# Three late chunks, a shorter gathered part of layer 2, and its chunk transfers on ScalarE's queue

## Chip, cores and metric

The kernel runs on one core of a Trainium2 chip. The metric is the device time of one execution in microseconds (us). Before the change the median of three runs is 3162.39 us (3161.69 to 3169.01).

## What is computed

A graph of 6250 nodes with 206250 edges, sorted by destination, goes through two graph convolutions and a projection, and then each node goes through a mixture of eight experts, two for each node:

```python
deg_out = segment_sum(edge_weight, src); deg_in = segment_sum(edge_weight, dst)
norm = edge_weight * rsqrt(deg_out[src] * deg_in[dst] + EPS)
def gcn_layer(x, W, b):
    xt = x @ W                                        # 256 x 256
    agg = segment_sum(xt[src] * norm[:, None], dst)
    return relu(agg + b)
h6 = gcn_layer(layernorm(x), W6, b6)
h7 = gcn_layer(h6, W7, b7)
x = x + h7 @ Wp + bp
...
xn = layernorm(layernorm(x)) * gamma + beta           # then top 2 of 8 experts
y += (gelu(xn @ W1[e] + b1[e]) @ W2[e] + b2[e]) * weight_of_e
return x + y
```

All of it is float32.

## The kernel before

**Tiles, chunks and groups.** The sorted edges are cut into tiles of 128; eight tiles are a group, 202 groups in all. A layer's weighted sum over edges is made in two ways. The *gathered part*: for a group, GpSimd gathers the source rows of the table of the layer, one indirect DMA for each tile (L977, `gathers`), into a ring of four group buffers (`RING`). TensorE multiplies them with one-hot matrices from VectorE (`sums`, L2111) and, after each second group, adds up the rows of both in `combine` (L2124), for which it needs the copy of the sums by ScalarE (`copy_sums`, L1760) and one row that SyncE fetches from the sums stored before (`carry_row`, L731). The *dense part*: the first tiles are turned into chunks. A chunk is 30 or 31 tiles whose destinations lie in one window of 128 rows; its adjacency matrix, 128 rows for each of 49 blocks of sources, stands in one of two buffers (`adj`), 26 KB for each partition. VectorE makes the one-hots of a tile (`tile_one_hots`, L1294 and L1295), TensorE multiplies them (`build_tile`, L2083), and VectorE adds the result into the buffer (`add_tile`, L1323). `apply_step` (L2098) then multiplies the chunk with the table in 27 steps, 49 blocks in all, and the buffer is zeroed behind it by ScalarE (`zero_chunk`, L1771).

**Layer 1** applies 24 chunks (`CHUNKS`, 736 tiles) while it gathers the other 110 groups. Each of the 24 matrices is stored to memory, for layer 2 needs the same ones. The loop covers 96 groups (`LOOP_GROUPS`). Then come 14 tail slots, `for k in range(TAIL)`, each with a group; the last chunk is applied in the first four, and pairs of 128-row blocks are finished from the fifth on (`tail_pairs`): root of the degree, scaling, transposes, relu, product with W7, table of layer 2. In the same slots *late chunks* are built (`EXTRAS`) which layer 1 does not apply: their rows are gathered in layer 1, but layer 2 uses them as chunks. There are two, of 18 and 30 tiles (`LATE_CT`), built in the slots 0 to 3 and 4 to 11. ScalarE stores the first in slot 5 and loads chunk 0 in slot 7, SyncE stores the second between the layers. Layer 2's gathers start when the whole table has been stored (`p_stored`).

**Layer 2** applies 26 chunks and gathers 104 groups. It goes by slots, one group in each (`layer2_slots`). The first 8 chunks (`SHORT`) have three slots each, the other 18 four, which makes 96 slots (`CHUNKS_END`); eight slots follow with a group and no chunk. From slot 10 on the stages of the 25 pairs are laid into the slots, six slots for a pair (`STARTS`, `pair_starts`): projection, layer norms, router, list of the experts. In the slot where chunk c starts (j == 0), SyncE's program stores the sums of chunk c - 1 (`store_rows`), issues the load of chunk c + 1 (`load_chunk`, L770), fetches the row carried between chunks (`carry_chunk`, L761) and, for an even group, the one carried between groups (L731). All these go through SyncE's one DMA queue, in this order. Then 105 expert blocks follow, of which the first 18 share slots with the last pairs.

Every engine executes its instructions in order. An engine that waits holds back all that stands behind it in its program.

Of the kernel before, what the change touches and what calls it, by code (L numbers as in the profile page):

```python
# [34 lines left out]
LATE_CT, SHORT = (18, 30), 8  # L35
# [11 lines left out]
MERGED_PAIRS = 11,  # L47
# [6 lines left out]
PARTS_OUT = 16  # L54

OFFS, CHUNK_OFFS = 16, 32

# [27 lines left out]
def gnn_moe_kernel(nc, A):  # L85
# [37 lines left out]
    with ExitStack() as ctx:  # L123
# [83 lines left out]
        SC_W = 5 * DTX  # L207
# [256 lines left out]

        block = ctx.enter_context(nc.Block())

# [103 lines left out]
        def group_no(L, n):  # L570
# [3 lines left out]
        EXTRAS = [range(DT + LATE_CT[0] * k // FIRST_EXTRA, DT + LATE_CT[0] * (k + 1) // FIRST_EXTRA)  # L574
                  for k in range(FIRST_EXTRA)]
        EXTRAS += [range(DT + LATE_CT[0] + LATE_CT[1] * k // 8, DT + LATE_CT[0] + LATE_CT[1] * (k + 1) // 8)
                   for k in range(8)]
        EXTRAS += [range(0)] * (TAIL - len(EXTRAS))
        FIRST_STORED_AT, FIRST_LOADED_AT = FIRST_EXTRA + 1, FIRST_EXTRA + 3
# [19 lines left out]
        def chunks_for(b):  # L599
            return next(c for c in range(ALL) if chunk_start(c) >= tiles_before((b + 1) * PT * P) + CT // 2)  # L600
# [74 lines left out]
        def _(sp):  # L675
# [92 lines left out]
            def load_chunk(c):  # L768
                sp.wait_ge(applied[1], SLICES * (c - 1))
                sp.dma_start(adj[:, c % 2].rearrange("p h w -> p (h w)"), chunks[c * P:(c + 1) * P, :]  # L770
                             ).then_inc(chunk_in[c % 2], 16)

# [49 lines left out]
            with sp.If(bad < 1):  # L822
# [59 lines left out]
                store_chunk(ALL - 1)  # L882

                def layer2_slot(n, c, j, g, stages):
# [11 lines left out]
                    if c and j == 0:  # L896
                        store_rows(1, c - 1)
                        if c + 1 < ALL:
                            load_chunk(c + 1)
                        carry_chunk(1, c)  # L900
# [834 lines left out]
        def _(act):  # L1735
# [116 lines left out]
            def layer2_slot(n, c, j, g, stages):  # L1852
                if c and j == 0:
# [17 lines left out]
                for i, _, s in stages:  # L1871
                    if s == 2:
                        half_tanh(i)

# [31 lines left out]
            def load_chunk(c):  # L1906
                act.wait_ge(chunk_stored, 16 * (CHUNKS + c + 1))
                act.dma_start(adj[:, c].rearrange("p h w -> p (h w)"), chunks[c * P:(c + 1) * P, :]
                              ).then_inc(chunk_in[c], 16)
# [56 lines left out]
            with act.If(bad < 1):  # L1966
# [21 lines left out]
                for k in range(TAIL):  # L1988
# [8 lines left out]
                    if k == FIRST_STORED_AT:  # L1997
                        act.wait_ge(added, DT + LATE_CT[0])
                        act.dma_start(chunks[CHUNKS * P:(CHUNKS + 1) * P, :], adj[:, CHUNKS % 2].rearrange("p h w -> p (h w)")
                                      ).then_inc(chunk_stored, 16)  # L2000
# [482 lines left out]
```

## Time and profile before

| | |
|---|---|
| median of three runs | 3162.39 us |
| the profiled execution | 3166.45 us |
| its span, first to last instruction | 3164.5 us |
| mean granted TensorE clock | 0.919 of full speed |
| busy: TensorE, GpSimd, VectorE, ScalarE | 83%, 62%, 60%, 27% |
| gathers (L977) | 1712, from 373.4 us on |
| chunk applications (L2098) | 4900 matmuls, 50 chunks |

One execution is profiled. Times in its rows are microseconds from the start of the span, busy times are of instructions that ran. A float32 matmul counts as two instructions. "x <- y" behind a line names the tile that is written and the tile that is read. What ended an idle time is inferred from semaphore events.

### The profile page before, as it was taken

To read this page: it belongs to the slowest core of one execution; us is meant where nothing else is said; L and a number is where in the kernel's file an instruction comes from. 1 tells how busy PE (TensorE), PEld (TensorE's weight loads), DVE (VectorE), ACT (ScalarE), POOL (GpSimd) and SP (SyncE) were. 2 spreads that over 40 slices of the span, in tenths; PEclk is the share of its full clock that TensorE was granted. 3 is DMA by queue.
4 is the path that set the end of the run, shared out by engine and by line. 5 is a ranking of instruction groups with operands and counts; after the bars stand their busy time and mean duration, and the time that the engine had idled before them with its cause. 6 is when DMAs were issued, how large, how long until landed. Compare 5 with 4: busy or idle time off the path is not lost. (4 is left out here: it accounts for less than half of the span.)

```text
span 3164.5 us, 53882 instructions
## 1 busy us (share of the span) xinstructions
PE 2631.7 (83%) x16919; PEld 2013.0 (64%) x16919; DVE 1911.0 (60%) x6028; ACT 861.5 (27%) x2052; POOL 1963.4 (62%) x1932
## 2 busy tenths in 40 slices
PE   4567479999999999995589988888888875899995
PEld 3456247676667776663466766666666553889984
DVE  9999878888888887864203545455545446522210
ACT  5677611122121222112201100000011001456652
POOL 0000277777777777777477777777777763467763
PEclk8699789999999999997899999899999885999997
DMA  4001355566665655668666766666666663344444
GB/s 129 0 22 43 115 166 181 201 204 203 199 203 193 195 188 191 203 199 276 207 201 226 259 213 213 194 217 215 226 220 221 219 226 93 60 66 71 70 67 115
DMA packets 197506, 530.79 MB, mean 168 GB/s; under 512 B 39338, under 2 KB 129247, under 8 KB 190463
## 3 DMA queue, kind: packets, MB, share of 16 engines
q0 software_dynamic: 102336, 252.47, 30.5%
q1 hardware_dynamic: 92174, 256.65, 22.4%
q10 hardware_dynamic: 2736, 18.48, 1.5%
q8 instruction: 131, 2.15, 0.3%
q14 instruction: 129, 1.05, 0.1%
HBM read 377.61 MB, written 156.24 MB: 169 GB/s over the span
## 5 line engine op out<-in xcount | busy, mean ns | idle before, releaser
L977 POOL DMA_INDIRECT arena<-table,src_i x1712 | 1673.7, 978 | 596.2 <-issue 514.5
L2098 PE MATMUL bank<-arena 128*128 128x257 f32 x4900 | 1246.5, 391 | 3.1 <-ACT zcd L1784 2.4
L2098 PEld LDWEIGHTS bank<-arena 128*128 128x128 f32 x4900 | 901.7, 194 | 202.5 <-issue 83.4
L2083 PE MATMUL bank<-arena 128*128 128x294 bf16 x2352 | 426.2, 295 | 49.6 <-DVE arena L1295 32.3
L1323 DVE TENSOR_TENSOR arena<-arena,bank 128x294 f32 x784 | 357.3, 456 | 176.4 <-PE bank L2083 164.9
L1295 DVE SCALAR_TENSOR_TENSOR arena<-iota_f,arena 128x256 f32<-128x256 f32 x784 | 366.8, 468 | 0.0
L2083 PEld LDWEIGHTS bank<-arena 128*128 128x128 bf16 x2352 | 226.4, 100 | 207.9 <-DVE arena L1323 46.3
L2111 PE MATMUL bank<-arena,s_all 128*32 128x257 f32 x3424 | 246.2, 408 | 75.1 <-DMA arena<-table,src_i 68.4
L1771 ACT COPY arena<-zero 128x2144 f32<-128x2144 f32 (+1 forms) x104 | 156.3, 1533 | 398.3 <-DMA chunks<-arena 335.9
L1003 POOL DMA_INDIRECT acc<-arena x105 | 178.7, 1702 | 126.6 <-ACT arena L1897 97.6
L1294 DVE TENSOR_SCALAR arena<-iota_key,arena 128x294 bf16<-128x294 bf16 x784 | 242.7, 310 | 0.0
L2055 PE MATMUL bank<-arena 128*128 128x150 bf16 x1616 | 152.6, 256 | 107.6 <-DVE arena L1143 72.2
L1582 DVE COPY arena<-arena 128x1024 f32 x105 | 76.2, 733 | 261.9 <-PE bank L2297 245.7
L968 POOL PARTITION_ALL_REDUCE bad_all<-bad_f x1 | 0.4, 380 | 358.4 <-DVE bad_f L1285 358.4
L2055 PEld LDWEIGHTS bank<-arena 128*128 128x128 bf16 x1616 | 132.7, 109 | 128.9 <-DVE arena L1143 107.3
L2297 PE MATMUL bank<-arena 128*128 128x128 f32 x1680 | 211.0, 280 | 0.0
L2306 PE MATMUL bank<-arena 128*128 x840 | 203.1, 384 | 8.8 <-ACT arena L1897 8.8
L2111 PEld LDWEIGHTS bank<-arena,s_all 128*32 128x32 f32 x3424 | 93.5, 114 | 178.6 <-DMA arena<-table,src_i 76.1
L1760 ACT COPY zs<-bank 127x257 f32<-127x257 f32 x107 | 40.1, 375 | 608.2 <-PE bank L2111 607.3
L2297 PEld LDWEIGHTS bank<-arena 128*128 128x128 f32 x1680 | 202.2, 197 | 0.1
L2306 PEld LDWEIGHTS bank<-arena 128*128 128x128 f32 x840 | 153.3, 193 | 28.3 <-issue 10.5
L990 POOL DMA_INDIRECT arena<-rows_x,arena x105 | 109.2, 1040 | 85.1 <-DVE arena L1487 34.0
(238 smaller groups left out, 2678.3 us busy)
## 6 DMA issues: line engine op xcount, KB each, us to landing
chunks<-arena SPq DMA_DIRECT2D x25, 3283.0 KB, 12.7
arena<-chunks SPq DMA_DIRECT2D x24, 3283.0 KB
arena<-table,src_i POOLq DMA_INDIRECT x1712
zsum<-zc SPq DMA_DIRECT2D x107, 128.5 KB, 3.2
zrow<-zsum SPq DMA_DIRECT2D x50, 257.0 KB, 4.7
arena<-in_W ACTq DMA_DIRECT2D x16, 512.0 KB, 16.9
rows_x<-arena SPq DMA_DIRECT2D x25, 264.0 KB
arena<-chunks ACTq DMA_DIRECT2D x2, 3283.0 KB
```

The lines of the kernel that those rows point to most:

```text
L977: pool.indirect_dma_start(gat[:, r, j, 0:D], None, table[L], bass.IndirectOffsetOnAxis(ap=src_i[:, col:col + 1], axis=0)).then_inc(gathere ...
L1003: pool.indirect_dma_start(acc, bass.IndirectOffsetOnAxis(ap=row_e[:, j:j + 1], axis=0), ye[:, j % 2], None, compute_op=ALU.add).then_inc(y ...
L1294: dve.tensor_scalar(ohk[:, r], iota_key[:, 0:KEYS], key[:, t:t + 1], None, ALU.is_equal)
L1295: dve.scalar_tensor_tensor(out=words[:, r], in0=bc_mid(iota_f[:, :], 2), scalar=lo_f[:, t:t + 1], in1=bc_in(w_words[:, t], P), op0=ALU.is_ ...
L1323: dve.tensor_tensor(win, win, ps_b[t % len(ps_b)].rearrange("p (h w) -> p h w", w=TW), ALU.add).then_inc(added, 1)
L1771: done = act.copy(adj[:, c % 2, first:first + whole], zero[:, :].unsqueeze(2).broadcast_to([P, whole, AWID]))
L2055: last = pe.matmul(ps_do, oh_lo[:, r, j // TI, :, j % TI], whi[:, r, j // TI, :, :, j % TI].rearrange("p i n -> p (i n)"), start=False, st ...
L2083: last = pe.matmul(ps_b[t % len(ps_b)], halves[:, t % OH_RING, word, :, half], ohk[:, t % OH_RING], start=(i == 0), stop=(i == 2))
L2098: last = pe.matmul(ps_ap, adj[:, c % 2, h, 0:P], xp[:, h], start=(h == 0), stop=(h == XB_ALL - 1))
L2111: last = pe.matmul(ps_seg[q * WIN:(q + 1) * WIN, :], s_mat[:, r, q * HQ + j], gat[:, r, q * HQ + j], start=(j == 0 and not second), stop=( ...
L2297: last = pe.matmul(ps_h[j % 2][:, c], w1_e[:, j % W1_RING, k, c * P:(c + 1) * P], xeT[:, j % 2, k], start=(k == 0), stop=(k == KD - 1))
L2306: last = pe.matmul(ps_y, hs[:, j % 2, c], w2_of(e, c), start=(c == 0), stop=(c == HC - 1))
```

## The change

`LATE_CT` becomes (31, 31, 18): 816 tiles are chunk tiles for layer 2 instead of 784, in 27 chunks, and layer 2 gathers 100 groups, 32 gathers fewer. The late chunks are built in the tail slots 0 to 3, 4 to 8 and 9 to 12. The first 16 chunks of layer 2 have three slots (`SHORT`), the other 11 four: 92 slots, and eight without a chunk as before. Pair 12 takes the place of pair 11 as the one whose rows lie in both parts, and pairs of the dense part may start three tiles (`ROW_TILES`) behind their last row where it was half a chunk. Since 27 is odd, layer 2 holds chunk c in buffer (c + 1) % 2.

The transfers of layer 2's chunks leave SyncE's queue. ScalarE issues them at the end of its part of a chunk's first slot, each as seven transfers of up to seven blocks, 3.75 KB for each partition. ScalarE stores the first late chunk in slot 5, the second in slot 10, zeroes the buffer of the third in slot 8, and loads chunk 0 in slot 12. SyncE stores the third, in seven pieces as well. The constants of layer 2 share an area that shrinks from 3920 to 3640 words.

```diff
-LATE_CT, SHORT = (18, 30), 8
+LATE_CT, SHORT = (31, 31, 18), 16
...
-MERGED_PAIRS = 11,
+MERGED_PAIRS = 12,
+ROW_TILES = 3
...
+PIECE = 7
...
+        PIECES = [(h, min(h + PIECE, XB_ALL)) for h in range(0, XB_ALL, PIECE)]
...
+        def stores_until(c):
+
+            return 16 * (min(c, CHUNKS) + len(PIECES) * max(c - CHUNKS, 0))
...
+        def chunk_pieces(c, buffer):
+            return [(chunks[c * P:(c + 1) * P, h * AWID:k * AWID], adj[:, buffer, h:k].rearrange("p h w -> p (h w)"))
+                    for h, k in PIECES]
...
-        EXTRAS = [range(DT + LATE_CT[0] * k // FIRST_EXTRA, DT + LATE_CT[0] * (k + 1) // FIRST_EXTRA)
-                  for k in range(FIRST_EXTRA)]
-        EXTRAS += [range(DT + LATE_CT[0] + LATE_CT[1] * k // 8, DT + LATE_CT[0] + LATE_CT[1] * (k + 1) // 8)
-                   for k in range(8)]
+        LATE_TURNS = FIRST_EXTRA, 5, 4
+        EXTRAS = [range(chunk_start(CHUNKS + i) + LATE_CT[i] * k // n, chunk_start(CHUNKS + i) + LATE_CT[i] * (k + 1) // n)
+                  for i, n in enumerate(LATE_TURNS) for k in range(n)]
         EXTRAS += [range(0)] * (TAIL - len(EXTRAS))
-        FIRST_STORED_AT, FIRST_LOADED_AT = FIRST_EXTRA + 1, FIRST_EXTRA + 3
+        STORED_AT = FIRST_EXTRA + 1, sum(LATE_TURNS[:2]) + 1
+        ZEROED_AT, FIRST_LOADED_AT = sum(LATE_TURNS[:2]) - 1, TAIL - 2
...
-            return next(c for c in range(ALL) if chunk_start(c) >= tiles_before((b + 1) * PT * P) + CT // 2)
+            return next(c for c in range(ALL) if chunk_start(c) >= tiles_before((b + 1) * PT * P) + ROW_TILES)
...
-            def load_chunk(c):
-                sp.wait_ge(applied[1], SLICES * (c - 1))
-                sp.dma_start(adj[:, c % 2].rearrange("p h w -> p (h w)"), chunks[c * P:(c + 1) * P, :]
-                             ).then_inc(chunk_in[c % 2], 16)
...
-                store_chunk(ALL - 1)
+                sp.wait_ge(chunk_stored, stores_until(ALL - 1))
+                sp.wait_ge(added, DTA)
+                for rows, part in chunk_pieces(ALL - 1, (ALL - 1) % 2):
+                    sp.dma_start(rows, part).then_inc(chunk_stored, 16)
...
                         store_rows(1, c - 1)
-                        if c + 1 < ALL:
-                            load_chunk(c + 1)
                         carry_chunk(1, c)
...
+                if c and c + 1 < ALL and first_of_chunk:
+                    load_next(c + 1)
...
             def load_chunk(c):
-                act.wait_ge(chunk_stored, 16 * (CHUNKS + c + 1))
-                act.dma_start(adj[:, c].rearrange("p h w -> p (h w)"), chunks[c * P:(c + 1) * P, :]
-                              ).then_inc(chunk_in[c], 16)
+                for rows, part in chunk_pieces(c, (c + 1) % 2):
+                    act.dma_start(part, rows).then_inc(chunk_in[c % 2], 16)
+
+            def load_first(c):
+                act.wait_ge(chunk_stored, stores_until(CHUNKS + c + 2))
+                load_chunk(c)
+
+            def load_next(c):
+                act.wait_ge(applied[1], SLICES * (c - 1))
+                if c >= CHUNKS:
+                    act.wait_ge(chunk_stored, stores_until(ALL))
+                load_chunk(c)
...
+                    if k in STORED_AT:
+                        c = CHUNKS + STORED_AT.index(k)
+                        act.wait_ge(added, chunk_start(c + 1))
+                        for rows, part in chunk_pieces(c, c % 2):
+                            act.dma_start(rows, part).then_inc(chunk_stored, 16)
+                    if k == ZEROED_AT:
+                        act.wait_ge(chunk_stored, stores_until(CHUNKS + 1))
+                        for i in range(SLICES):
+                            zero_chunk(ALL - 1, *slice_bounds(i))
                     if k == FIRST_LOADED_AT:
-                        load_chunk(0)
+                        load_first(0)
...
-                load_chunk(1)
+                load_first(1)
...
-                    pe.wait_ge(chunk_in[c % 2], 16 * (c // 2) + 16)
+                    pe.wait_ge(chunk_in[c % 2], 16 * len(PIECES) * (c // 2 + 1))
```

## Rows read from the trace of the kernel before

**Rows 1.** Busy time by stretch: us, then each engine's busy us (instructions), clock, DMA share.

```profile
1471.00:1530.00 59.00, 45.33 (x323) 31.30 (x326) 33.48 (x111) 22.55 (x66) 37.13 (x39) 0.91 0.79 242
1530.00:1555.00 25.00, 11.79 (x47) 8.21 (x39) 5.75 (x19) 4.89 (x14) 0.00 (x0) 0.80 0.20 69
...
1570.00:1839.00 269.00, 242.96 (x1360) 187.41 (x1360) 90.37 (x396) 22.66 (x58) 202.61 (x213) 0.94 0.69 228
1839.00:2583.00 744.00, 643.59 (x3727) 478.80 (x3727) 373.16 (x1642) 71.51 (x191) 547.43 (x574) 0.94 0.66 212
2583.00:2680.00 97.00, 43.05 (x212) 23.14 (x212) 56.22 (x262) 7.99 (x21) 39.25 (x41) 0.55 0.53 171
```

**Rows 2.** GpSimd's gathers of layer 2: ns min/median/max, first and last start; idle before them.

```profile
L977 POOL DMA_INDIRECT arena<-table,src_i x832: 940/946/1427, 1555.3 to 2638.9; - x167
...
  issue: 248.3, 814
  PE bank L2111: 41.6, 17
```

**Rows 3.** TensorE's chunk matmuls (L2098), 1570 to 2583: busy us, weight loads busy.

```profile
sum 1013.00, PE 611.60 PEld 488.76; mean PE 305.80 PEld 244.38
```

**Rows 4.** TensorE's waits, 1839 to 2583, then 1599 to 1839: total, times, longest.

```profile
PE bank L2124 <- DMA zs<-zsum: 35.3, 15, 5.1
...
PE bank L2111 <- DMA arena<-table,src_i: 7.4, 1, 7.4
...
PE bank L2124 <- DMA zs<-zsum: 3.0, 2, 2.2
```

**Rows 5.** Groups of instructions by form, TensorE, 1560 to 2640: busy, mean ns.

```profile
L2111 PE MATMUL bank<-arena,s_all 128*32 128x257 f32 x1600 | 115.3, 408 | 27.2 <-DMA arena<-table,src_i 25.0 <-issue 2.1
...
L2124 PE MATMUL bank<-zs,arena 128*128 128x257 f32 x100 | 33.2, 415 | 38.7 <-DMA zs<-zsum 38.2 <-ACT zs L1760 0.5
```

**Rows 6.** Timeline of SyncE's queue, tail of layer 1 and layer 2: start, us, issue.

```profile
1482.22 0.30 SPq L731 DMA_DIRECT2D zs<-zsum  x1
...
2133.43 0.43 SPq L770 DMA_DIRECT2D arena<-chunks  x1
...
2138.74 0.30 SPq L731 DMA_DIRECT2D zs<-zsum  x1
```

**Rows 7.** Timeline of TensorE, tail of layer 1 and layer 2; the wait before in brackets.

```profile
1466.30 3.78 PE L2150 MATMUL bank<-w,hT 128*128 128x256 f32 x8 [16.62 <-ACT hT L1805]
...
1471.05 1.08 PE L2111 MATMUL bank<-arena,s_all 128*32 128x257 f32 x16
...
1479.35 1.07 PE L2111 MATMUL bank<-arena,s_all 128*32 128x257 f32 x16
...
1496.45 1.20 PE L2124 MATMUL bank<-zs,arena 128*128 128x257 f32 x2 [8.72 <-DMA zs<-zsum]
1497.57 1.94 PE L2111 MATMUL bank<-arena,s_all 128*32 128x257 f32 x16
...
1528.61 1.94 PE L2111 MATMUL bank<-arena,s_all 128*32 128x257 f32 x32
...
2148.02 0.67 PE L2124 MATMUL bank<-zs,arena 128*128 128x257 f32 x2 [3.80 <-DMA zs<-zsum]
```

**Rows 8.** Timeline of ScalarE: zeroing, the load of chunk 0, one issue of weights.

```profile
1424.56 3.86 ACT L1771 COPY arena<-zero 128x2144 f32<-128x2144 f32 x2
...
1480.50 0.36 ACTq L1908 DMA_DIRECT2D arena<-chunks  x1
...
2581.42 0.45 ACTq L1917 DMA_DIRECT2D arena<-in_W  x1
```

**Rows 9.** Timeline of VectorE: two adds of tiles that follow each other.

```profile
1501.19 0.45 DVE L1323 TENSOR_TENSOR arena<-arena,bank 128x294 f32 x1
...
1502.17 0.45 DVE L1323 TENSOR_TENSOR arena<-arena,bank 128x294 f32 x1
```

**Rows 10.** Timeline of VectorE in the setup: small operations.

```profile
362.92 3.20 DVE L1250 SCALAR_TENSOR_TENSOR arena<-arena 128x416 f32<-128x416 f32 x16
```

More of the change, by code:

```diff
@@ L54 @@
 PARTS_OUT = 16
+PIECE = 7
 OFFS, CHUNK_OFFS = 16, 32
+L2_WORDS = 3640
 TINY_EW = 2.0 ** -15
@@ L206, in gnn_moe_kernel @@
         DTX = DTA
-        SC_W = 5 * DTX
+        SC_W = max(4 * DTX, 2 * DTX + E8, L2_WORDS)
         arena = sb("arena", [P, GAT_W + OHK_W + PART_W + CM_W + OHG_W + XP_W + A_W + SC_W])
@@ L1852, in layer2_slot @@
             def layer2_slot(n, c, j, g, stages):
-                if c and j == 0:
+                first_of_chunk = j == 0
+                if c and first_of_chunk:
                     copy_chunk(1, c - 1)
@@ L1996, in _ @@
                         zero_behind(CHUNKS - 1, 3)
[L1997 to L2000, printed above, removed]
+                    if k in STORED_AT:
[7 more added lines that the diff above has]
+                            zero_chunk(ALL - 1, *slice_bounds(i))
                     if k == FIRST_LOADED_AT:
-                        load_chunk(0)
+                        load_first(0)
                     tail_pairs(TAIL_PAIRS[k])
@@ L2097, in apply_step @@
                         pe.wait_ge(chunk_carried, 16 * (L * CHUNKS + c + 1))
-                    last = pe.matmul(ps_ap, adj[:, c % 2, h, 0:P], xp[:, h], start=(h == 0), stop=(h == XB_ALL - 1))
+                    last = pe.matmul(ps_ap, adj[:, (c + L) % 2, h, 0:P], xp[:, h], start=(h == 0), stop=(h == XB_ALL - 1))
                 if step in ZERO_BEHIND:
```

## The prediction, made before the changed kernel was run

> **What bounds the kernel now.** I read the time by stretches first [rows 1]. They cut the span where the work changes: the end of layer 1 (1471 to 1530), the hand-over to layer 2 (1530 to 1555), layer 2's slots that apply chunks (1570 to 2583) and its last eight slots (2583 to 2680); the expert blocks behind them are not touched. In the chunk slots TensorE is busy 243 of 269 us and 644 of 744 us, GpSimd 203 and 547. So two engines are close to the bound, and the waits must say which one it is. Layer 2's 832 gathers run from 1555.3 to 2638.9 [rows 2]: 1.302 us each. Of this, 41.6 us in 17 pieces are waits for TensorE to release a gather buffer; without them a gather would follow the other every 1.253 us, 10.03 us for a group of eight and 1043 us in all. The other way round, TensorE waited for gathers 7.4 us once after 1599, and not at all between 1839 and 2583 [rows 2, 4]. TensorE sets the pace in layer 2 and the gathers are 4% behind it. That is the fact on which everything hangs: a group less saves the gathers 10 us, but the path only what TensorE spends on a group.
>
> **Layer 2, the new chunk and the missing groups.** The change turns four groups (32 tiles) into chunk work: 27 chunks in 92 slots for 26 chunks in 96, and 8 slots without a chunk behind them in both. A chunk costs TensorE 611.6 / 26 = 23.5 us [rows 3]. A group costs 115.3 / 100 = 1.15 us and, every second time, a combine of 33.2 / 50 = 0.66 us [rows 5]. The sum is +23.5 - 4 x 1.15 - 2 x 0.66 = +17.6 us for TensorE. The gathers would save 32 x 1.254 = 40 us, which is worth nothing as long as TensorE is last: 92 slots of gathers need 923 us, TensorE's 27 chunks about 1000. By the rule of `pair_starts`, 21 pairs start in the chunk slots in both. The last eight slots have the same pairs at the same distance from the last chunk, so I take them at nothing; the cover of that zero is that the last gather starts at 2638.9 and the stretch ends at 2680, 40 us of room [rows 1, 2].
>
> **Layer 2, the loads on another queue.** In its slot with a new chunk SyncE issues a load of 3.3 MB and, 5.3 us later, the one row that carries the sum over a group's edge (`carry_row`); TensorE's combine then waits for that row, here 3.8 us, until 2148.02, 9 us after the issue of a transfer of 1 KB [rows 6, 7]. Between 1839 and 2583 this happened 15 times for 35.3 us, about once for each of 18 chunks, and before that twice for 3.0 us [rows 4]. With the load on ScalarE's queue the row is no longer behind it. But the trace also shows that another queue alone is no cure: at 1480.50 ScalarE issued a load, SyncE issued a carried row at 1482.22, and the combine waited 8.7 us for it, to 1496.45 [rows 6 to 8]. What should help is the cut into seven pieces of 3.75 KB for each partition in place of one of 26 KB. A small transfer then takes turns with short packets instead of long ones. I take 5/6 of the 38.3 us back: -32 us, with bounds of 0 (nothing helps) and -38. The moved load also leaves SyncE's queue earlier in the slot, so the room of the carried row before its combine rises; that is why I choose near the full gain.
>
> The Trainium skill, DMA: Bandwidth & Descriptors, section Rules for kernel authors, says that spreading transfers over the queues of several engines does not help bandwidth and saves issue time only. By that alone the carry waits would stay and the sum would come out 32 us higher. 
>
> **ScalarE pays for it.** One issue took 0.45 us [rows 8], seven take 3.2 us, at the end of the slot in which a chunk starts. Behind it on ScalarE stands the copy of the sums of the next slot, on which TensorE's combine waits, where that slot is odd and a router's tanh had held ScalarE (five such slots by the schedule). I price them at 1 us: +5, bounds 0 and 26 x 3.2 / 2 = +40 (every second load on the path), near the low end because ScalarE is busy 94 of 1013 us there. The load starts up to 13 us later than now and has two slots of about 11 us left. The load issued at 2133.43 was through by 2148.02, for the row behind it on its queue had landed: 14.6 us at most. So I see no wait for it, but its margin is only some 5 us. The gather wait of 7.4 us in slot 4 stands beside such a load; short packets should give back 4 us. Layer 2 together: +17.6 - 32 + 5 - 4 = -13 us.
>
> **Layer 1's tail.** It has 14 slots, and 32 more tiles must be built and added there: 7.75 a slot instead of 4.5 in the first four, 6.2 instead of 3.75 in the next five, 4.5 in the last four. A tile costs VectorE 0.98 us from one add to the next [rows 9]. In the first four slots VectorE and TensorE have room; I take 13 tiles x 0.35 us = +4.6 us. In slot 5 TensorE waits 16.6 us for a pair that is behind a long transfer [rows 7]: the extra tiles disappear there, but the 4.6 us move that transfer too. In slots 6 to 8, 2.45 tiles x 0.98 us = 2.4 us each: slot 6 took 1471.05 to 1479.35, 8.3 us, with VectorE just in time for the pairs, so they count: +7.2. The wait of 8.7 us in slot 7 goes, because chunk 0 is no longer loaded then: -8.7. Slot 8 gets a whole buffer to zero, four pieces at 1.93 us (two took 3.86); the slot's pair needs ScalarE behind them, while VectorE's tiles hide about half: +3.5, bounds 0 and 7.7. Slots 9 to 12: +2 for the tiles, +1 for the new tiles of slot 12, +1.5 for issuing a store in slot 10. Sum: 4.6 + 7.2 - 8.7 + 3.5 + 2 + 1 + 1.5 = +11 us.
>
> The hand-over then takes 25 us from the last sums (1528.61) to the first gather of layer 2, a chain of small transfers and short operations with DMA at 20% [rows 1, 7]. Chunk 0's load, until now over long before, falls into it: ScalarE's issue of 3.2 us stands ahead of the last copy of sums, and carried row, store and two pair loads share the DMA engines with it: +4 us, bounds +1 and +12 (the row that waited 8.7 us). GpSimd has nothing to do meanwhile, so all of this is on the path: +15 us. The third late chunk also adds about five small VectorE operations to the setup ahead of the first gather, 0.2 us each [rows 10]: +1 us.
>
> **Sum.** The profiled execution took 3166.45 us (span 3164.5), 4.1 above the median of 3162.39. Against its own time: 3166.45 + 1 + 15 - 13 = 3169.5, and from the median 3165.4 us. A run of this kernel can't tell a change under 0.3% (9.5 us) from none.
>
> **Rivals.**
> 1. *Transfers stop holding up anything, and the tail swallows its tiles.* For it: the two large waits of the tail, 16.6 and 8.7 us, are both waits for small transfers beside large ones; if the pieces shorten the first as well, slots 6 to 8 start earlier. Against it: the first is behind a transfer on its own queue. It would give the tail +3 instead of +15, layer 2 the full -38 and -4 more: 3162.4 + 1 + 3 - 23 = 3143 us.
> 2. *The carry waits stay (the other side).* The load still takes the DMA engines for some 10 us, whatever its queue; a carried row and a stored sum that meet it wait as now, in layer 2's chunk slots. For it: the 8.7 us beside ScalarE's load. Against it: the length of the packets. Price: 32 us at full, 3197 us; with half of it 3181. The sum is zero where 8% of the waits stay, and over +9.5 us from 35% on.
> 3. *Layer 1 runs over.* Slots 5 to 12 become VectorE's and ScalarE's (zeroing, issuing, roots of pairs in one queue), each slot takes 11 us instead of 9, and GpSimd is stopped by full buffers: +15 more, 3180 us. For it: at 1471 TensorE has eight groups left and GpSimd five (37.13 us of gathers at 0.95), and the ring allows a lead of four [rows 1, 7].
> 4. *The gathers were the bound after all*, and each saved gather counts: 3162 + 16 - 40 = 3138 us. Against it: the waits of GpSimd for TensorE.
> That the change does nothing is excluded by the number of gathers (1712 becomes 1680).
>
> **Chances.** Forecast 0.42; rival 1 0.22; rival 2 0.15; rival 3 0.13; rival 4 0.08. Rivals 1 and 4 are faster by over 0.3%, rivals 2 and 3 slower: faster 0.30, same 0.42, slower 0.28. The forecast's own range is 3155 to 3175. The range reaches from a little below rivals 1 and 4 to the middle of rivals 2 and 3: 3136 to 3191; outside it lie the full price of rival 2 and tail gains beyond those named.
>
> **What the new profile would show.** Right: combine's waits for carried rows fall from 38 to about 6 us; 27 chunks of 23.5 us; the chunk slots of layer 2 take about 1000 us instead of 1013; GpSimd's first gather of layer 2 comes some 16 us later, near 1571; GpSimd's waits for TensorE grow, to 60 us or more. Wrong: a wait of the chunk's matmuls for its load, copies of sums that come late behind ScalarE's issues, waits for carried rows that stay, or a layer 2 that starts before 1560 or after 1585.

## The result, and the profile after

The changed kernel took 3198.1 us against 3165.7 us for the kernel before in the same runs: 1.0096 times as long, 95% interval 1.0071 to 1.0120. I had forecast +3 us and it is +32, outside my range, at the full price of rival 2 (3197 us). The profiled execution took 3194.2 us, 27.8 more than the one of before, and splits into +0.1 us up to the first gather of layer 1, +18.1 up to the first gather of layer 2 (predicted +15), +13.2 from there to the last gather, -3.5 behind it.

The same stretches as in [rows 1], with the same columns: tail of layer 1, hand-over, layer 2's chunk slots, its last eight slots. The line under them is the sum row of the chunk matmuls over the third stretch and answers [rows 3].

```profile
1485.00:1541.00 56.00, 42.96 (x276) 28.42 (x274) 36.63 (x122) 23.76 (x59) 29.11 (x30) 0.94 0.73 220
1541.00:1573.00 32.00, 13.97 (x55) 9.23 (x52) 6.68 (x21) 4.77 (x13) 0.00 (x0) 0.68 0.44 157
1588.00:2616.00 1028.00, 898.94 (x5117) 683.28 (x5117) 458.68 (x2026) 92.71 (x244) 725.25 (x757) 0.94 0.67 214
2616.00:2711.00 95.00, 43.72 (x212) 23.13 (x212) 56.25 (x257) 7.99 (x21) 35.72 (x39) 0.57 0.50 160
...
sum 1028.00, PE 631.94 PEld 509.44; mean PE 631.94 PEld 509.44
```

The gathers of layer 2 (answers [rows 2]), then TensorE's waits in 1590 to 2600 of the new kernel (total us, times, longest):

```profile
L987 POOL DMA_INDIRECT arena<-table,src_i x800: 940/946/1432, 1573.5 to 2670.3; - x160
...
  PE bank L2138: 95.3, 26
...
PE bank L2151 <- DMA zs<-zsum: 35.3, 5, 9.4
PE bank L2160 <- DVE zr_all L1372: 26.8, 14, 5.9
...
PE bank L2138 <- DMA arena<-table,src_i: 7.8, 3, 4.4
PE bank L2151 <- ACT zs L1770: 5.5, 5, 1.4
```

and the same window of the kernel before, for the comparison with all experiments below:

```profile
PE bank L2124 <- DMA zs<-zsum: 38.2, 17, 5.1
PE bank L2133 <- DVE zr_all L1362: 23.4, 12, 7.3
```

To be seen: 27 chunks of 631.94 / 27 = 23.4 us, as forecast. GpSimd waits for TensorE 95 us where it waited 42, so TensorE still sets the pace, as forecast. But the combines (`zs<-zsum`) still wait 35 us for carried rows, in 5 pieces of up to 9.4 us in place of 17 of up to 5.1. This is the line on which I had put -32 us. It didn't move in total, yet its shape changed, so it is not simply "the same waits as before".

One of the five, in order of time (start, us, instruction, the wait before it):

```profile
2306.83 0.37 ACT L1794 COPY zcd<-bank 128x257 f32<-128x257 f32 x1 [3.10 <-PE bank L2125]
2306.84 5.42 ACTq L1921 DMA_DIRECT2D arena<-chunks  x7
2308.61 0.40 SPq L828 DMA_DIRECT2D acc<-arena  x1
2309.79 1.03 SPq L766 DMA_DIRECT2D zsum<-zcd  x1
...
2324.43 0.31 SPq L775 DMA_DIRECT2D arena<-zsum  x1
2325.71 0.30 SPq L745 DMA_DIRECT2D zs<-zsum  x1
...
2327.27 1.20 PE L2151 MATMUL bank<-zs,arena 128*128 128x257 f32 x2 [9.38 <-DMA zs<-zsum]
...
2329.80 0.69 DVE L1372 TENSOR_SCALAR zr_all<-zrow,mv 128x256 f32<-128x256 f32 x2 [14.12 <-DMA zrow<-zsum]
```

ScalarE copies a chunk's finished sums (`zcd`) and issues the seven pieces of the next chunk's load in the same breath. SyncE stores those sums 3 us later, because it stood in `store_acc` (L828, 256 KB, issued just before). The store, 128 KB, now shares the DMA engines with a load of 3.3 MB whose issue began 3 us before it and ended 1.4 us behind it; it took 13.9 us from issue to landing. SyncE waits in `carry_chunk` until it has landed, and behind that wait stand the chunk's row (L775), the group's carried row (L745) and the load of a pair's rows (`zrow`, "root rows" below, on which `zr_all` and TensorE's transposes wait). The row itself is quick: 1.6 us from its issue to the combine. In the kernel before, store and load stood in one queue with the store ahead. SyncE's waits for the landing of this store, 2100 to 2600, before and after:

```profile
SPq L744 <- DMA zsum<-zcd: 28.3, 10, 3.9
```
```profile
SPq L758 <- DMA zsum<-zcd: 73.3, 11, 12.9
```

2.8 us each before, 6.7 after, 12.9 at most. (This is the half of the stage that shows it best: over 1590 to 2570 it is 2.7 us before, 24 times, and 4.9 after, 25 times.) So the theory for the experiments: **the load, on a queue of its own, overtakes the store whose landing releases the small transfers; what the pieces give the row, the late store takes.** Rivals: the price is the queue itself, or the seven issues; the pieces do nothing or do harm; the long hand-over is chunk 0's load.

### The profile page after: what moved, and what is told of

It is laid out like the page before. It is cut to its first block and busy times, and to the rows that moved or that the text cites. A ratio compares the mean times of both kernels' runs of the same rounds, so it can differ in the third digit from the quotient of the medians.

```text
span 3192.4 us, 54455 instructions
## 1 busy us (share of the span) xinstructions
PE 2657.1 (83%) x17045; PEld 2034.4 (64%) x17045; DVE 1938.2 (61%) x6119; ACT 866.5 (27%) x2055; POOL 1937.1 (61%) x1900
## 5 line engine op out<-in xcount | busy, mean ns | idle before, releaser
L987 POOL DMA_INDIRECT arena<-table,src_i x1680 | 1648.7, 981 | 651.9 <-issue 502.6
L2125 PE MATMUL bank<-arena 128*128 128x257 f32 x4998 | 1266.6, 391 | 2.7 <-ACT zcd L1794 2.0
L2125 PEld LDWEIGHTS bank<-arena 128*128 128x128 f32 x4998 | 920.3, 194 | 204.7 <-issue 82.6
L2110 PE MATMUL bank<-arena 128*128 128x294 bf16 x2448 | 442.5, 294 | 56.9 <-DVE arena L1305 32.6
L1333 DVE TENSOR_TENSOR arena<-arena,bank 128x294 f32 x816 | 371.9, 456 | 178.6 <-PE bank L2110 164.1
L1305 DVE SCALAR_TENSOR_TENSOR arena<-iota_f,arena 128x256 f32<-128x256 f32 x816 | 382.2, 468 | 0.0
L1304 DVE TENSOR_SCALAR arena<-iota_key,arena 128x294 bf16<-128x294 bf16 x816 | 252.4, 309 | 0.0
L2324 PEld LDWEIGHTS bank<-arena 128*128 128x128 f32 x1680 | 201.9, 197 | 0.1
L2333 PEld LDWEIGHTS bank<-arena 128*128 128x128 f32 x840 | 151.8, 191 | 25.1 <-issue 7.6
```

What stands on the lines that cost most here:

```text
L987: pool.indirect_dma_start(gat[:, r, j, 0:D], None, table[L], bass.IndirectOffsetOnAxis(ap=src_i[:, col:col + 1], axis=0)).then_inc(gathere ...
L1304: dve.tensor_scalar(ohk[:, r], iota_key[:, 0:KEYS], key[:, t:t + 1], None, ALU.is_equal)
L1305: dve.scalar_tensor_tensor(out=words[:, r], in0=bc_mid(iota_f[:, :], 2), scalar=lo_f[:, t:t + 1], in1=bc_in(w_words[:, t], P), op0=ALU.is_ ...
L1333: dve.tensor_tensor(win, win, ps_b[t % len(ps_b)].rearrange("p (h w) -> p h w", w=TW), ALU.add).then_inc(added, 1)
L2110: last = pe.matmul(ps_b[t % len(ps_b)], halves[:, t % OH_RING, word, :, half], ohk[:, t % OH_RING], start=(i == 0), stop=(i == 2))
L2125: last = pe.matmul(ps_ap, adj[:, (c + L) % 2, h, 0:P], xp[:, h], start=(h == 0), stop=(h == XB_ALL - 1))
```

## The experiments

All times are medians; ratios are against runs of the kernel before on the same chip. The runs are from several chips, so two rows are best compared by their ratios (0.001 is 3.2 us); differences of medians, which the text gives, can be off by up to 7 us. "The changed kernel" has 27 chunks, "the kernel before" 26. "Pieces" are those of `PIECE`, which also cuts the loads of the chunks 0 and 1 and, with 27 chunks, the stores of the late chunks in layer 1's tail.

| run | chunks | layer 2's loads | us | ratio (95%) |
|---|---|---|---|---|
| before | 26 | SyncE, whole | 3160 to 3166 | 1 |
| c_queue_only | 26 | ScalarE, 7 pieces | 3163.0 | 0.9995 (0.9975 to 1.0016) |
| e_queue_wait | 26 | the same, held for the store | 3153.5 | 0.9960 (0.9946 to 0.9975) |
| e4 | 26 | held, 13 pieces | 3183.3 | 1.0074 (1.0050 to 1.0098) |
| g_before_nocarry | 26 | SyncE, whole; no carried rows | 3136.2 | 0.9923 (0.9894 to 0.9951) |
| i_row_first | 26 | SyncE, whole, behind the row | 3201.1 | 1.0114 (1.0078 to 1.0150) |
| after | 27 | ScalarE, 7 pieces | 3198.1 | 1.0096 (1.0071 to 1.0120) |
| d_after_store | 27 | held, 7 pieces | 3173.1 | 1.0027 (1.0009 to 1.0044) |
| d4 | 27 | held, 13 pieces | 3190.1 | 1.0103 (1.0065 to 1.0141) |
| d14 | 27 | held, 4 pieces | 3202.1 | 1.0119 (1.0086 to 1.0152) |
| d1_after_store_one | 27 | held, whole | 3216.6 | 1.0154 (1.0115 to 1.0194) |
| b_one_piece | 27 | ScalarE, whole | 3253.9 | 1.0263 (1.0212 to 1.0315) |
| a_sp_queue | 27 | SyncE, whole | 3219.3 | 1.0167 (1.0130 to 1.0204) |
| a7_sp_pieces | 27 | SyncE, 7 pieces | 3244.7 | 1.0258 (1.0231 to 1.0284) |
| f_after_nocarry | 27 | as after; no carried rows | 3182.9 | 1.0065 (1.0039 to 1.0090) |
| h_load0_late | 27 | as after; chunk 0's load late | 3199.6 | 1.0118 (1.0078 to 1.0158) |

### The order of load and store

d_after_store: the changed kernel, and ScalarE waits for the landing of the store before it issues the load.

```diff
                 if c and c + 1 < ALL and first_of_chunk:
+                    act.wait_ge(zd_stored[1], 16 * c)
                     load_next(c + 1)
```

> The changed kernel, in which ScalarE waits, before it issues the load of chunk c + 1, until SyncE's store of the sums of chunk c - 1 has landed. Theory (collision): the carried rows come in time, waits for them fall from 35 to under 8 us, the chunk slots of layer 2 take about 1000 instead of 1028 us, total 3170 us. Rival (bandwidth: the load delays whatever runs beside it, whenever it starts): waits of 20 us or more stay, total 3190 us. Rival (ScalarE pays): the wait holds up ScalarE by 4 us for each chunk, total 3200 us or more.

25 us came back (22 by the ratios), as the theory said. GpSimd's gathers of layer 2, TensorE's waits in 1590 to 2600, and SyncE's for the store in 1590 to 2570:

```profile
L987 POOL DMA_INDIRECT arena<-table,src_i x800: 940/946/1429, 1576.7 to 2647.6; - x160
...
PE bank L2161 <- DVE zr_all L1372: 41.8, 18, 5.9
...
PE bank L2152 <- DMA zs<-zsum: 10.6, 5, 4.3
...
SPq L758 <- DMA zsum<-zcd: 74.0, 25, 4.1
```

SyncE waits for the store 3.0 us on the mean and 4.1 at most; the waits for carried rows fall from 35 to 11 us (I had expected under 8). The chunk slots of layer 2 take 999 us (1591.5 to 2590.5), as expected. A slot with a new chunk now reads:

```profile
2262.12 0.36 SPq L766 DMA_DIRECT2D zsum<-zcd  x1
...
2266.65 0.31 SPq L775 DMA_DIRECT2D arena<-zsum  x1
2267.94 0.30 SPq L745 DMA_DIRECT2D zs<-zsum  x1
...
2269.40 3.43 ACTq L1922 DMA_DIRECT2D arena<-chunks  x6
...
2277.14 0.59 PE L2152 MATMUL bank<-zs,arena 128*128 128x257 f32 x2
```

The combine at 2277.14 has no wait. Holding the load does two things at once: the store is not overtaken, and the carried row (2267.94) goes out ahead of the load as well. No run separates the two; in the slot shown for the changed kernel the row took 1.6 us of a chain of 17. The waits for root rows (`zr_all`) have risen from 27 to 42 us: part of what one small transfer gains, another now pays.

The first row says more. From layer 2's first gather to its last it is now 1070.9 us, 12.7 less than before (1083.6), where the prediction had -13 for layer 2. What keeps the kernel behind the one before is all ahead of it: the first gather comes at 1576.7, 21 us later than before.

f_after_nocarry: is it only the carried row that the late store costs? Layer 2's carried rows are left out (the partial sum over the edge of two groups is missing).

```diff
-                sp.dma_start(zs[P - 1:P, :], row).then_inc(carried, 16)
+                if L == 0:
+                    sp.dma_start(zs[P - 1:P, :], row).then_inc(carried, 16)
...
-                    pe.wait_ge(carried, 16 * (s + 1))
+                    pe.wait_ge(carried, 16 * (min(s, GROUPS[0] // 2 - 1) + 1))
```

> The changed kernel without the carried rows of layer 2's groups (SyncE issues none, the combines do not wait; the partial sum over the edge of two groups is left out). In the kernel before, leaving them out took 38 us of waits and 30 us of time. Theory (in the changed kernel the carried row is what the late store of sums delays): 3165 to 3175 us, all of d_after_store's gain or a little more. Rival (the late store holds up more than the rows, the loads of root rows for one): 3180 to 3190 us.

The rival was right: 15 us (10 by the ratios), though 35 us of waits are gone, and 10 less than the order gives back. The late store holds up more than the rows: SyncE still waits 116.8 us for it (122.6 in the changed kernel, 74.0 with the load held), and TensorE's waits for root rows rose to 44.5 us.

### Queue alone, in the kernel before

c_queue_only: before's chunks; the only edit is who loads and in how many pieces.

```diff
-                        if c + 1 < ALL:
-                            load_chunk(c + 1)
...
+                if c and c + 1 < ALL and first_of_chunk:
+                    load_next(c + 1)
```

> The kernel before, with only the queue part of the change: layer 2's chunks loaded by ScalarE in seven pieces at the end of the first slot of a chunk. Late chunks, slots and layer 1 as before. Theory (collision): waits for carried rows stay near 38 us, but in half as many and twice as long waits; total 3160 to 3172 us. Rival (the pieces free the carried rows): waits of 5 us, total 3130 to 3140 us. Rival (ScalarE pays): copies of sums late, total 3180 us or more.

The total is as expected, but not the way to it. I had expected the row's waits to stay at 38 us; they fell to 9, as the prediction wanted, and still nothing was gained (TensorE's waits in 1590 to 2600):

```profile
PE bank L2145 <- DVE zr_all L1362: 40.1, 20, 7.4
...
PE bank L2136 <- ACT zs L1760: 9.6, 9, 1.8
PE bank L2136 <- DMA zs<-zsum: 8.9, 2, 5.6
```

-29 us of waits for rows came with +17 for root rows, +9 for copies of sums that ScalarE makes late behind its issues, and 8 us more TensorE busy time (866.3 for 858.0 in 1590 to 2570) at a granted clock of 0.93 for 0.94. The sum is +5. From the first chunk matmul of layer 2 to the last, the same 5052 matmul instructions took 1008.6 us for 1007.5: 9.5 us more of busy time, 8.4 less idle. The run moved by -3, within the noise. In the kernel before, then, the moved queue is worth nothing; the prediction had given it -31 us (-32 + 5 - 4).

g_before_nocarry prices these waits by themselves (the edit of f_after_nocarry in the kernel before, the same sums missing).

> The kernel before without the carried rows of layer 2's groups: SyncE issues none and the combines do not wait for them (the partial sum over the edge of two groups is left out). It prices the waits by themselves. Theory (a wait of TensorE for a row is path, as in my sum): the 38 us come back in full or nearly, 3125 to 3135 us. Rival (a saved wait turns into another: a later wait of the same slot, or a lower granted clock of TensorE): 3150 to 3166 us, with more waits for root rows, or the clock of the chunk stage below 0.94.

24 us by the ratio, 30 by the medians: nearer to the theory (3136 us for its 3125 to 3135) than to the rival, a little short of full. GpSimd's waits for TensorE fell from 41.6 to 10.9 us, and TensorE's for the gathers rose from 7.4 to 15.9. The gathers, 4% behind, had nearly become the bound, which would explain why not all came back:

```profile
  PE bank L2112: 10.9, 6
```

e_queue_wait: c_queue_only with the load held for the store.

> The kernel before with ScalarE's queue for layer 2's loads, in seven pieces (as in c_queue_only), and the load held until SyncE's store of the finished sums has landed. Theory (the load overtakes the store; what waits for the store then comes late): it gains over c_queue_only what the same wait gained in the changed kernel, so 3140 to 3155 us against 3165.8 of the kernel before, with waits of the combine for carried rows under 12 us and waits for root rows no longer than before (about 25 us). Rival (in the kernel before's chunk stage another thing sets the pace, such as TensorE's clock, and every wait taken away comes back elsewhere): 3160 to 3168 us.

3153.5 us, inside the theory's range: 12.5 us or 0.4% faster than before, the interval clear of 1. It beats both kernels and is the version to keep. Waits for carried rows are no longer among TensorE's seven largest in 1590 to 2600; those for root rows are:

```profile
PE bank L2146 <- DVE zr_all L1362: 38.3, 19, 6.1
...
PE bank L2137 <- ACT zs L1760: 12.9, 9, 3.1
```

So I was wrong on the second half of that expectation: root rows waited 38 us, not 25. The gain over c_queue_only is 9 us (11 by the ratios) where it was 25 in the changed kernel, and the two intervals only just touch. Here the store was overtaken less, as SyncE's waits for it in 1590 to 2570 show: 90.9 us in c_queue_only and 63.4 with the load held, 27 us less, where it was 49 less in the changed kernel (122.6 and 74.0).

i_row_first asks whether order alone, on one queue and uncut, will do: the load goes behind the carried row where the slot has one.

```diff
                         store_rows(1, c - 1)
-                        if c + 1 < ALL:
+                        row_first = g is not None and g % 2 == 0
+                        if c + 1 < ALL and not row_first:
                             load_chunk(c + 1)
                         carry_chunk(1, c)
+                        if row_first:
+                            carry_row(1, g)
+                            if c + 1 < ALL:
+                                load_chunk(c + 1)
+                            g = None
```

> The kernel before, with SyncE's load of a chunk issued behind the carried row of the same slot in place of ahead of it (where the slot has one, about every second chunk), one whole transfer, one queue. Theory (only the order of small and large transfers decides who waits; neither another queue nor a cut is needed): the waits for carried rows fall from 38 to about 10 to 20 us and the time to 3145 to 3155 us. Rival (each saved wait comes back as another, as in c_queue_only where waits for root rows rose by 15 us): 3158 to 3168 us.

Both were wrong: 3201 us, +40. The waits for carried rows are gone from TensorE's list, and the root rows of the following slots pay 69 us more (92.6 for 23.4). The store of a group's sums now stands behind the whole load in the queue, and SyncE waits for its landing before it fetches a pair's root rows (L776): 80.9 us in eight waits, 29.8 before.

```profile
PE bank L2139 <- DVE zr_all L1368: 92.6, 19, 11.4
...
SPq L776 <- DMA zsum<-zc: 80.9, 8, 13.8
```

### The cut

b_one_piece is the changed kernel, d1_after_store_one is d_after_store, both with whole transfers (`PIECE = 49` for `PIECE = 7`).

> The changed kernel with every cut load and store whole again (one transfer of 26 KB for each partition in place of seven), still on ScalarE's queue. If it is the cut that lets small transfers through, as my prediction had it, the carry waits of layer 2's chunk stage rise from 35 us to over 60 and the time to 3220 us or more. If it is the order of load and store that decides, the cut is worth little: 3190 to 3202 us. Rival (pieces are harmful: the small store advances by about one packet for each short packet of the load, but the load lasts 17 us in place of 11): 3180 to 3190 us.

> As d_after_store (the changed kernel, ScalarE's load held until the store of the finished sums has landed), but whole in place of in seven pieces. Only the carried row and loads of pairs and root rows meet the load now. If the cut helps the small transfers that it meets: slower than d_after_store by 8 us or more, 3181 to 3200 us, with carry waits back at 30 us. If the order alone decides: 3168 to 3178 us.

+56 us without the cut, and +43 where the order is right; both are slower than I expected. The cut matters more than anything else in this change, and "the order alone decides" has fallen. Not all of it is layer 2: the stores of the tail are whole here too, and the first gather of layer 2 comes 11.8 us later in b_one_piece and 4.4 in d1_after_store_one. Nor is all of it what I had said it would be: in b_one_piece the waits for carried rows rose to 47.9 us, not to over 60. In d1_after_store_one the small transfers wait all over the slot (1590 to 2600):

```profile
PE bank L2161 <- DVE zr_all L1372: 44.8, 17, 8.5
PE bank L2240 <- DVE off_i L1470: 35.0, 4, 11.3
...
PE bank L2152 <- DMA zs<-zsum: 17.1, 5, 4.1
```

In 1590 to 2570 TensorE is idle 139.7 of 980 us (105.1 in d_after_store), and its clock is 0.92 for 0.95.

d14 has four pieces in place of seven, d4 and e4 thirteen (`PIECE = 14`, `PIECE = 4`).

> As d_after_store, but loads cut into four parts (7.5 KB for a partition and packet) in place of seven. Measured at the ends: 26 KB packets 3217 us, 3.75 KB packets 3173. Theory A (what a small transfer waits for is a packet of the load in front of each of its own, so the price grows with the length of a packet): 3180 to 3188 us. Theory B (any cut that is not whole is enough, four issues cost ScalarE less than seven): 3165 to 3175 us.

> As d_after_store with the load cut into thirteen pieces of at most 4 tiles (2.1 KB for a partition). By the packet's length (26 KB 3217, 7.5 KB 3202, 3.75 KB 3173): 3160 to 3168 us, waits for root rows under 38 us. By the load's length (more packets, a longer load, and 13 issues of ScalarE at 0.8 us each): 3176 to 3195 us, with waits for copies of sums by ScalarE of 15 us or more.

> As e_queue_wait (the kernel before with ScalarE's queue, seven pieces, load held until the store landed: 3153.5 us), with thirteen pieces of 2.1 KB. By the packet's length: 3140 to 3150 us. By the load's length and ScalarE's issues: 3156 to 3170 us; ScalarE's copies of sums already cost TensorE 12.9 us with seven pieces and would cost 25.

The profile counts one packet for each partition's row of a transfer: c_queue_only has 3328 packets of over 8 KB fewer than the kernel before, 128 for each of the 26 loads. Packets of 26, 7.5, 3.75 and 2.1 KB gave 3217, 3202, 3173 and 3190 us. Four pieces came out slower than both theories had it, so the price doesn't grow in proportion with the packet: most of the gain lies between 7.5 and 3.75 KB. But it doesn't lie in waits alone. Over the chunk matmuls of layer 2 the same 5082 matmul instructions took d14 35 us longer than d_after_store, and 20 of these are busy time (908.9 us for 888.6) at a clock of 0.92 for 0.95. The waits for root rows were 44.8, 46.3 and 41.8 us with one, four and seven pieces; only thirteen brought them down, to 21.5, which speaks for the packet's length and against the load's as what holds these transfers up (a part may only be that slots start later). What ends the gain is ScalarE. d4's waits and one of its issues:

```profile
PE bank L2152 <- ACT zs L1770: 42.1, 10, 5.7
PE bank L2161 <- DVE zr_all L1372: 21.5, 15, 4.6
...
2323.24 8.24 ACTq L1922 DMA_DIRECT2D arena<-chunks  x13
```

Thirteen issues keep ScalarE 7 to 9 us, and TensorE waits 42 us (49.5 in e4) for copies of sums behind them. e4, at 3183 us, is slower than both of its theories. (d4's profiled execution took 3175 us, its other four 3188 to 3192; the waits may be a little low.) Seven is the best of the sizes tried.

a_sp_queue puts the load back into SyncE's queue, whole, right behind the store, with the changed kernel's chunks; a7_sp_pieces does so in seven pieces.

> The changed kernel with layer 2's loads from chunk 2 on given back to SyncE's queue, one transfer each, right behind the store of the chunk's sums; late chunks, slots and the rest as changed. Theory (collision): in the changed kernel ScalarE's load overtakes SyncE's store of the chunk's sums in every second chunk, and the carried row comes late; total waits for carried rows are 35 us as before. Giving the queue back only changes their shape: one wait of 2 to 4 us for each chunk that starts in an even slot, some 35 us in all, total 3195 to 3202 us, first gather of layer 2 still near 1573. Rival (ScalarE's issues and the seven pieces themselves cost the time): 3180 us or less. Rival (the late chunks cost nothing): 3165 us.

> As a_sp_queue (the changed kernel, layer 2's loads on SyncE's queue right behind the store of the finished sums), but in seven pieces. It tells the cut from the queue. On one queue the pieces do not let a row through that stands behind them. Theory: 3210 to 3225 us, as a_sp_queue's 3219, with seven issues of SyncE ahead of the row; the cut only works together with a queue of its own. Rival (the cut is good in itself): 3190 to 3200 us.

The cut is no gain in itself: on SyncE's queue it makes things worse, 3245 for 3219 us, 20 us above what I expected. The carried row stands behind the pieces in the same queue and behind seven issues (3.9 to 5.1 us), and TensorE's waits for it are 40.3 us for 25.2. a_sp_queue was also above its range: without the new queue the third late chunk cost 53 us, not the 34 of my sum. Its granted clock was 0.88 in 2150 to 2400 and 0.85 in 2400 to 2600 (before: 0.95 and 0.90), beside longer waits in 2150 to 2600, 22.7 us for carried rows (14.9 before) and 22.1 for `off_i` (6.3). The trace splits it in part: over the chunk matmuls the same 5082 matmul instructions took 1047.3 us for 1019.0 in the changed kernel, and of these 28 us 20 are TensorE busy longer (915.2 for 895.4) and 8 idle. Why the clock was lower, no run shows.

### The hand-over

h_load0_late loads chunk 0 behind the last pair, together with chunk 1, in place of two slots earlier.

> The changed kernel, in which chunk 0 is loaded behind the last pair's output (with chunk 1's load) instead of in tail slot 12, so nothing of it falls into the hand-over between the layers. Theory: of the 32 us between the last sums of layer 1 and the first gather of layer 2 some 7 us are the load's (three for its issue ahead of the copy of sums, the rest for the carried row's transfer); layer 2 then starts near 1565 instead of 1573. TensorE needs chunk 0 about 15 us after that, when its load has just landed: total 3188 to 3195 us. Rival (the hand-over is long for another reason): start stays at 1573 and chunk 0 comes late, total 3200 to 3210 us.

3199.6 us, and layer 2's first gather at 1572.4, not 1565: by the time the theory has fallen. The trace is kinder to it. The chain of the hand-over begins with SyncE's last store of a group's sums (L754), whose landing releases the carried row (L745), whose landing releases a combine. First the changed kernel, then h_load0_late:

```profile
1540.95 3.10 ACTq L1921 DMA_DIRECT2D arena<-chunks  x4
1542.12 0.36 SPq L754 DMA_DIRECT2D zsum<-zc  x1
...
1551.34 0.30 SPq L745 DMA_DIRECT2D zs<-zsum  x1
...
1552.97 1.20 PE L2151 MATMUL bank<-zs,arena 128*128 128x257 f32 x2 [10.55 <-DMA zs<-zsum]
```
```profile
1544.70 0.36 SPq L754 DMA_DIRECT2D zsum<-zc  x1
...
1547.52 0.30 SPq L745 DMA_DIRECT2D zs<-zsum  x1
```

The store takes 9.2 us to land where ScalarE's load is being issued around it (from 1539.59 to 1544.05), and 2.8 us without: the same collision as in layer 2. From that store to the first gather it is 31.3 us in the changed kernel and 27.7 here, so 3.6 of the 6.4 us come back at the gather. But this execution reached the store 2.6 us later, and in the five kernels whose code is the same up to there (after, d_after_store, f_after_nocarry, a_sp_queue, a7_sp_pieces) the first gather of layer 2 came between 1573.5 and 1579.6, so one execution each can't weigh 4 us; the total says only that they aren't seen in the end.

## Why the prediction was wrong, point by point

**The bound** was right. TensorE set the pace; GpSimd's waits for it were forecast at 60 us or more and are 95. (1083.6 - 41.6 is 1042 us or 1.252 for a gather, where I had 1043 and 1.253; nothing hangs on it.)

**Chunk and groups**, +17.6: right for a chunk, 23.4 us for 23.5. TensorE's busy time in the chunk slots rose by 898.9 - 886.6 = 12.3 us, idle time by 3, which holds the waits of the other terms too.

**The loads on another queue**, -32: this step failed. The waits for carried rows stood at 35.3 us, and the measured worth of the moved queue was -3 us in the kernel before. "I take 5/6 of the 38.3 us back" contains three claims. That short packets let a small transfer through: the cut is worth 43 to 56 us, though part of it lies in the tail and in busy time at a lower clock. That they do so for the row: true in c_queue_only (38 to 9 us). That a wait gone is time gone: half true. Waits for rows have a price, 30 us for 38, where nothing else takes their place (g_before_nocarry); with the load on ScalarE's queue root rows and copies of sums did take their place. What I left out altogether is the order: one queue had kept the store ahead of the load. "The moved load also leaves SyncE's queue earlier" was the sentence in which I should have asked what it leaves ahead of. Without the load SyncE does reach its row sooner, but not the landing for which it must wait first. Holding the load costs one line and gives 25 of the missing 29 us. The forecast of -13 us for layer 2 then came out (-12.7), though not by its terms: the rows gave back 28 us, root rows took 18 of them, and TensorE's clock was 0.95 for 0.94.

The rule that I quoted from the Trainium skill, DMA: Bandwidth & Descriptors, section Rules for kernel authors (spreading over queues helps no bandwidth), gave rival 2's time, and that time came. That the time fits is partly luck: rival 2 has the waits stay as they are, row and stored sum alike, where in fact the store came later than before, the waits changed their shape, and another pairing (c_queue_only) had hardly any left. The other, section Queues, rings and completion order, has each DMA engine serve its queues in turn, packet by packet. d1_after_store_one, d14 and d_after_store agree with what I drew from it: 3217, 3202 and 3173 us with shorter and shorter rows. No row here shows the turns themselves, and a packet of that section holds several descriptors, where the profile counts one packet for each row.

**ScalarE's issues**, +5: right in size, 5.5 us of waits in all (0.5 before). Seven issues take 3.4 to 5.5 us where I had 3.2. The load took less than the 14.6 us that I had as its bound: 13.5 in the median of a_sp_queue, whole and on SyncE's queue.

**Wait for gathers**, -4: not seen. The wait in slot 4 went from 7.4 to 4.4 us, but two others appeared, and all three are 7.8.

**Layer 1's tail**, +11: measured +10.9, up to SyncE's last store of a group's sums (1542.12 for 1531.25), but from wrong terms. TensorE's sums of the tail's groups in slots 6, 7, 8, 10 and 11, and the issue of a late store:

```profile
1470.05 1.08 PE L2138 MATMUL bank<-arena,s_all 128*32 128x257 f32 x16
...
1483.73 1.08 PE L2138 MATMUL bank<-arena,s_all 128*32 128x257 f32 x16
...
1494.42 1.08 PE L2138 MATMUL bank<-arena,s_all 128*32 128x257 f32 x16
...
1514.56 1.08 PE L2138 MATMUL bank<-arena,s_all 128*32 128x257 f32 x16
1516.48 6.26 ACTq L2023 DMA_DIRECT2D chunks<-arena  x4
1522.79 0.20 ACT L1809 ACTIVATE din<-din 128x2 f32<-128x2 f32 x1 [6.71 <-issue]
1523.95 1.04 PE L2160 MATMUL bank<-ident,zr_all 128*128 128x128 f32 x4 [3.84 <-DVE zr_all L1372]
...
1530.49 1.25 PE L2138 MATMUL bank<-arena,s_all 128*32 128x257 f32 x16
```

Slot 6 starts at 1470.05, 1 us earlier than before in place of 4.6 later: slot 5's wait took up the tiles. Slot 6 then takes 13.7 us for 8.3 (I had +2.4), slot 7 loses its wait of 8.7 as forecast, and slot 10 takes 15.9 us for 8.3 where I had priced the issue of a store at 1.5: four of its seven issues alone hold ScalarE 6.3 us, and the pair's roots stand behind them.

The +10.9 is one execution's, and so is the +18.1 up to layer 2: over the five kernels with this tail the first gather of layer 2 comes at 1576.6 on the mean, 21 us behind the one of the kernel before, where tail and hand-over had +15.

**Hand-over**, +4: measured +7.3 (31.3 for 24.0 us from that store to the first gather), inside the bounds of 1 and 12. 6.4 of it is the store's landing, 9.2 us for 2.8 (1531.25 to 1534.04 before); I had the load in the right place and looked at the row instead of the store ahead of it, the same oversight as in layer 2.

**Setup**, +1: +0.1.

The rest of the sum can't be called confirmed. The change minus its queue was +33.6 by my sum. From c_queue_only to the changed kernel it is +35 us, with the load held on both sides (e_queue_wait to d_after_store) +20, and with the loads left on SyncE's queue, whole (before to a_sp_queue), which is the sum's own case, +53. What a chunk costs depends on what its load collides with, so that +35 meets +33.6 is in part chance. It stays positive: the third late chunk doesn't pay in any pairing that was run, and with the load held what it costs is the later start of layer 2.

Of the rivals, the second gave the right time, and I had put it at 0.15 because of "the length of the packets", which was true and not the point.

## What to carry to other kernels

Before a transfer moves to a queue of its own, ask what the old queue's order protected: a small store whose landing releases others must stay ahead of the large load, by its queue or by a semaphore. A cut may pay too: cut a large transfer that shares the DMA engines with small ones on which the bound waits, but only on another queue, and only until the issuing engine's own work comes late. And price a wait that you remove by the next one in the same slot, not by its length.

## What I had not expected of the hardware

- A cut alone changed a kernel by 43 to 56 us (1.3 to 1.8%) at equal bytes, and between 7.5 and 3.75 KB packets by 29 us. In the profiled executions 20 of the 35 us between them in layer 2's chunk stage are TensorE's busy time for the same instructions.
- Seven DMA issues in a row took ScalarE 3.4 to 5.5 us, one alone 0.45 [rows 8]; four took 6.3 us while large transfers were in flight. The price of an issue is not fixed.
- SyncE waited at most 4.1 us for a 128 KB store with the load held, and up to 12.9 us where the load's issue had begun first on another queue.
- TensorE's granted clock in 1590 to 2570 was 0.93 to 0.95 in the kernels under 3200 us and 0.91 or 0.92 in the six above. Over the chunk matmuls of the 27-chunk kernels the same 5082 matmul instructions were busy for 889 to 901 us in the first and 902 to 919 in the others. So part of a wait's price may appear as slower matmuls. No run separates cause and effect here.
